# GpSimd waits for a gather's landing ahead of every third unit, and normalization batches of four up to the 44th unit, in a two-layer graph kernel

## The chip, the core and the metric

The kernel runs on one core of a Trainium2 chip. The metric is device time in microseconds (us) from start to end of one execution. Three runs of the kernel before took 1783.02, 1783.18 and 1783.73 us; the median is 1783.18 us. TensorE is written PE, VectorE DVE, ScalarE ACT, GpSimd POOL and SyncE SP, as in the profile.

## What is computed

There are 100,000 nodes with 128 features each and 50,000 edges, sorted by destination. Both layers normalize and clip the nodes' rows first.

```python
edge_index = jnp.stack([src, dst])
h = jnp.maximum(_layernorm(x, axis=-1), 0.0)
x = x + _L0_gnn_ref(h, relation_embedding, W1, b1, w2, edge_index, edge_type_200)
h = jnp.maximum(_layernorm(x, axis=-1), 0.0)
x = x + _L1_gnn_ref(h, src, dst)

# first layer, per edge and then per destination
triple = jnp.concatenate([x[src], x[dst], relation_embedding[edge_type]], axis=1)
c = triple @ W1 + b1
b = jax.nn.leaky_relu(c @ w2, SLOPE)
alpha = softmax of b over the edges of one dst
out = leaky_relu(segment_sum(c * alpha, dst))

# second layer: sum of feats[src] per dst, a node without edges keeps its own row
```

## The kernel before

The first layer goes through 261 units. A unit is three groups of 128 nodes (their rows are `xn`, loaded by SP, four units in one load) and up to two tiles of 128 edges. The source rows of the edges, `xe`, are fetched by POOL: `gather(u)` issues two indirect DMAs of 128 rows of 512 bytes for unit u (line 1112). `xe` has 16 slots, so `gather(u)` first waits until ACT has normalized unit u-16 (`L1.nrm`, line 1107).

All engines but POOL and SP walk through one loop of steps s, written out in full. Each issues its instructions strictly in the written order and meets the others by semaphores. In step s:

- DVE takes the statistics of some units further ahead (`stats`, line 1223; it waits for `x_in` and for `gathered`), makes the scalings of a batch once its last unit has been seen (`variances`, line 1231, and `ln_piece`, lines 1242, 1245, 1250, 1257), builds the selection matrices (`selT` 1310, `ot` 1320, `sel` 1333), runs the softmax of eight units in pieces, and adds the result to the nodes (1440, 1450).
- ACT copies messages out of PSUM (1562), makes the root of a batch's variances (`roots`, 1513 and 1515), normalizes unit s+2 (`norm`, five activations, 1527 and 1530), copies the turned tiles (1556) and unit s-15's sums (1568).
- PE turns unit s+1 (1601 to 1606), aggregates unit s-15 (1634 to 1637), and makes the messages of unit s (1618 to 1623).

The normalization batches are `LNB`: 2, 2, 4, 4 units, then thirty of 8, then 4, 2, 2, 1. `statistics_steps` spreads a batch's units over the steps between the end of the batch ahead and the step lo - 4, where lo is the batch's first unit. With batches of 8 behind each other the statistics of unit s+11 are taken in step s; with batches of 4 those of unit s+7. A gather can be at unit s+18 in step s, because of the 16 slots. At the very end the small batches ask for the last unit, 260, only in step 256.

SP brings `xn` and two tables every four steps and stores finished rows (lines 1006, 1026, 1038); these transfers and the gathers share the core's 16 DMA engines. The second layer begins when the first has stored all; it is not changed.

Of the kernel before, what the change touches and what calls it, by code (L numbers as in the profile page):

```python
# [16 lines left out]
def wait(engine, semaphore, value):  # L17

    if isinstance(value, int) and value <= 0:
        return  # L20
    engine.wait_ge(semaphore, value)
# [435 lines left out]
LB = 8  # L457
SB_ = 8
# [30 lines left out]
def gnn_two_layers(nc, x, src_e, dst_e, typ_e, rel, w1, b1, w2, out):  # L489
# [35 lines left out]
    with ctx:  # L525
# [95 lines left out]
        gathered = Ring(sem, "gathered", XE, 16 * UE)  # L621
# [63 lines left out]
        with ExitStack() as ctx1:  # L685
            block = ctx1.enter_context(nc.Block())

            @block.sync
            def _(sp):
                def first_x(q):  # L690
                    for rows_, g0, g1, np_ in parts_of(x, q):
                        sp.dma_start(xn[0:np_, q, g0:g1, :], rows_).then_inc(x_in.of(q), 16)

                for to, from_, landed in ((dsti, dst_e, k_dst), (srci, src_e, k_edge), (typi, typ_e, k_edge)):
                    sp.dma_start(to, from_.rearrange("o (p c) -> (o p) c", p=P)).then_inc(landed, 16)
                sp.dma_start(w1s[:, :, :], w1.rearrange("(a p) d -> p a d", p=P)).then_inc(k_in, 16)
                sp.dma_start(rels[:, 0, :], rel[0:P, :]).then_inc(k_in, 16)
                sp.dma_start(rels[0:RB, 1, :], rel[P:R, :]).then_inc(k_in, 16)
                sp.wait_ge(k_tab, 2)
                sp.dma_start(tab_d.rearrange("(p c) t -> p (c t)", p=P), tab.rearrange("p c t -> p (c t)")).then_inc(k_tabs, 16)  # L700
                sp.wait_ge(k_const, 1)
                sp.dma_start(nextp[0:P - 1, :], dst_e[:, EC:].rearrange("o (p c) -> (o p) c", c=EC)[:, 0:1],
                             allow_slow_non_contiguous=True).then_inc(k_in, 16)
                sp.dma_start(w2b[:, :], w2.partition_broadcast(P)).then_inc(k_in, 16)
                sp.dma_start(b1b[:, :], b1.partition_broadcast(P)).then_inc(k_in, 16)
                for k in range(TC):
                    sp.wait_ge(k_winl[1][k], 16)
                for q in range(2):
                    first_x(q)
                sp.wait_ge(k_places, UE)  # L710
                sp.dma_start(place_d.rearrange("(k p) s -> p k s", p=TU), plb).then_inc(k_out, 16)
                sp.wait_ge(k_types, UE)
                sp.dma_start(types_d.rearrange("(k p) s -> p k s", p=TU), tyb).then_inc(k_out, 16)
# [175 lines left out]
        with nc.If(flag == 0), ExitStack() as ctx2:  # L889
# [25 lines left out]
            def cut(sizes, most, total=NU):  # L915
                at, found = 0, []
                while at < total:
                    n = min(sizes[len(found)] if len(found) < len(sizes) else most, total - at)
                    found.append((at, at + n))
                    at += n  # L920
                return found

            def by_unit(batches):
                return {u: j for j, (lo, hi) in enumerate(batches) for u in range(lo, hi)}

            LNB, SMB = cut((2, 2, 4, 4) + 30 * (LB,) + (4, 2, 2, 1), LB), cut((), SB_)
            LN_OF, SM_OF = by_unit(LNB), by_unit(SMB)
            LNB2 = cut((1, 1, 2) + 30 * (LB2,) + (2, 1, 1), LB2, NU2)
            LN2_OF = by_unit(LNB2)
# [22 lines left out]
            def column(u, e):  # L952
                return (UE * (u // TU) + e) * TU + u % TU
# [4 lines left out]
            def xe_of(u):  # L958
                return xe[:, u % XE, :, :]
# [11 lines left out]
            def xe2_of(u):  # L971
                k = u % XE2
                return etiles[:, UT * k:UT * (k + 1), :] if k < 6 else xgroups[:, UT * (k - 6):UT * (k - 5), :]
# [4 lines left out]
            def tiles2(u):  # L978
                return UT - u % 2 - (u == NU2 - 1)
# [121 lines left out]
            @block.gpsimd  # L1101
            def _(pool):
                last_row = nc.gpsimd.to_reg(N - 1)

                def gather(u):
                    wait(pool, L1.nrm, u - XE + 1)
                    pool.sem_inc(turns, 1)
                    for e in range(UE):
                        if u < FIRST[e]:
                            continue  # L1110
                        j = column(u, e)
                        nc.gpsimd.indirect_dma_start(out=xe_of(u)[:, e, :], out_offset=None, in_=x,  # L1112
                                                     in_offset=bass.IndirectOffsetOnAxis(ap=idx_t[:, j:j + 1], axis=0),
                                                     bounds_check=last_row, oob_is_err=False
                                                     ).then_inc(gathered.of(u), 16)

                def gather2(u):
                    wait(pool, L2.y, u - XE2 + 2)
                    pool.sem_inc(turns, 1)
                    for k in range(tiles2(u)):  # L1120
                        j = NP2 * (u % 2 * UT + k) + u // 2
                        nc.gpsimd.indirect_dma_start(out=xe2_of(u)[:, k, :], out_offset=None, in_=x1_d,  # L1122
                                                     in_offset=bass.IndirectOffsetOnAxis(ap=idx2[:, j:j + 1], axis=0),
                                                     bounds_check=last_row, oob_is_err=False
                                                     ).then_inc(gathered.sems[u % XE2], 16)

                def window2(k):
                    if k == 0:
                        pool.wait_ge(k_borders, 2)
                    else:  # L1130
                        pool.wait_ge(k_rows2, k)
                    nc.gpsimd.indirect_dma_start(out=win2.rearrange("p c t -> p (c t)"), out_offset=None, in_=tab_d,
                                                 in_offset=bass.IndirectOffsetOnAxis(ap=at2[:, k:k + 1].bitcast(u32), axis=0)
                                                 ).then_inc(k_win2, 16)

                for u in range(NU):
                    if (u - T_WINDOW) % T_APART == 0 and 0 <= (u - T_WINDOW) // T_APART < ROUNDS:
                        window2((u - T_WINDOW) // T_APART)
                    gather(u)
                pool.wait_ge(s_c, NU)  # L1140
                nc.gpsimd.iota(row2, pattern=[[1, 4 * P]], base=0, channel_multiplier=0, allow_small_or_imprecise_dtypes=True
                               ).then_inc(k_row2, 1)
                for n in range(NQ - XS, NQ):
                    pool.wait_ge(stored.of(n), stored.count(n))
                pool.wait_ge(L1.nrm, NU)
                pool.wait_ge(k_tables2, ROUNDS)
                for u in range(NU2):
                    gather2(u)
# [608 lines left out]
```

## Time and profile before

| | |
|---|---|
| median of three runs | 1783.18 us |
| the profiled execution | 1799.49 us, its span 1795.3 us |
| busy over the span | PE 85%, DVE 82%, ACT 74%, POOL 65% |
| stretch 160 to 1000 us (224 units of the first layer) | PE 819.02 of 840 us, DVE 790.82, ACT 720.77, POOL 620.34 |
| granted TensorE clock | 1.00 in that stretch, 0.91 from 1100 to 1790 us |

Durations of rows are of the profiled execution. "Busy" of POOL leaves out the time between two instructions. A row of the timeline reads: start, duration, engine, line, operation, output<-input, count, and in brackets how long the engine had stood idle before it and what ended that.

### The profile page before, as it was taken

Reading aid. Unit: us, or ns where it says so; the run is one execution under the profiler, and the core shown is the slowest. Engines: PE = TensorE matmul, PEld = TensorE weight load, DVE = VectorE, ACT = ScalarE, POOL = GpSimd, SP = SyncE. Lnnn points to the kernel's source line nnn. Section 1 sums busy time; section 2 is a strip of 40 time slices with the busy share of each in tenths; the row PEclk is TensorE's granted clock in tenths of the full one; section 3 lists DMA queues with packets and bytes.
Section 4 is the critical chain, followed back from the end, with each engine's and each line's share of the span. In section 5 each row is a group of like instructions: output and inputs, shape, how many; then the busy total and the mean of one; then the engine's idle time right before and its main releaser. Section 6 shows DMA issues by size and latency. Waiting matters only on the chain.

```text
span 1795.3 us, 35038 instructions
## 1 busy us (share of the span) xinstructions
PE 1519.4 (85%) x12139; PEld 1346.7 (75%) x12139; DVE 1480.9 (82%) x4103; ACT 1335.6 (74%) x3492; POOL 1164.3 (65%) x994
## 2 busy tenths in 40 slices
PE   1379999999999999999999982687878778878787
PEld 0269999999999899998999982566656656656566
DVE  5548999999999899999999886677877787787786
ACT  0268888888888788888888952677766777777776
POOL 5756777777767677767777204666666666666661
PEclk9889999999999999999999996899899989989999
DMA  3543666666666566665666454477776677776754
GB/s 105 167 103 102 173 179 168 176 172 180 172 168 177 152 169 175 178 170 151 173 163 169 124 168 134 119 193 190 200 193 179 179 202 193 191 194 188 191 154 122
DMA packets 469368, 298.80 MB, mean 166 GB/s; under 512 B 35662, under 2 KB 438084, under 8 KB 469190
## 3 DMA queue, kind: packets, MB, share of 16 engines
q1 hardware_dynamic: 433942, 243.28, 49.2%
q0 software_dynamic: 35248, 53.28, 11.7%
q8 instruction: 95, 1.56, 0.4%
q14 instruction: 83, 0.68, 0.1%
HBM read 203.78 MB, written 104.34 MB: 172 GB/s over the span
## 4 chain that ended last, share of the span: by engine, by line
PE 47%; ACT 17%; POOL 10%; issue 9%; another core or an unknown queue 6%; DVE 5%; DMA 2%; SPq 0%; DVEq 0%; POOLq 0%; ACTq 0%
POOL xe L1122 8%; PE c_p L1618 5%; PE t_p L1604 5%; PE c_p L1619 5%; ACT an L1527 4%; ACT cs L1544 4%; PE c_p L1621 4%; PE t_p L1601 3%; ACT ae L1530 3%; PE t_p L1606 2%; PE t_p L1605 2%; PE y_p L1637 2%; ACT cs L1549 2%; PE y_p L1634 2%
## 5 line engine op out<-in xcount | busy, mean ns | idle before, releaser
L1112 POOL DMA_INDIRECT xe<-in_x,idx_t x516 | 681.6, 1321 | 264.6 <-issue 163.2
L1122 POOL DMA_INDIRECT xe<-x_d,idx x332 | 335.8, 1011 | 197.0 <-issue 128.2
L1223 DVE BATCH_NORM_STATS2 st<-xn 128x6 f32<-128x256 f32 x843 | 311.4, 413 | 39.4 <-DMA xn<-x_d,idx 27.2
L1527 ACT ACTIVATE an<-xn,nbias,rstd 128x128 f32<-128x128 f32 x783 | 326.9, 483 | 3.1 <-DVE nbias L1257 3.1
L1544 ACT ACTIVATE cs<-xn,nbias,rstd 128x128 f32<-128x128 f32 x782 | 310.3, 479 | 7.1 <-remote 7.1
L1223 DVE BATCH_NORM_STATS2 st<-xe 128x6 f32<-128x256 f32 x446 | 174.6, 412 | 108.0 <-DMA xe<-x_d,idx 96.2
L1530 ACT ACTIVATE ae<-xe,nbias,rstd 128x128 f32<-128x128 f32 x522 | 226.4, 483 | 0.0
L1618 PE MATMUL c_p<-w1a,th 128*128 128x129 f32 x1044 | 218.0, 290 | 9.9 <-issue 9.9
L1562 ACT ACTIVATE cs<-c_p 128x258 f32<-128x258 f32 x261 | 100.2, 384 | 147.6 <-remote 70.6
L1619 PE MATMUL c_p<-w1b,th 128*128 128x129 f32 x1044 | 203.8, 277 | 2.9 <-issue 2.9
L1333 DVE TENSOR_SCALAR sel<-row,plc_t,alpha 128x256 f32<-128x256 bf16 x522 | 194.3, 412 | 3.4
L1621 PE MATMUL c_p<-relk,ot 128*128 128x129 bf16 x1566 | 178.1, 222 | 2.4 <-issue 2.3
L1645 PE MATMUL y_p<-cs,ident 128*128 128x512 f32 x132 | 86.5, 791 | 97.0 <-issue 61.0
L1618 PEld LDWEIGHTS c_p<-w1a,th 128*128 128x128 f32 x1044 | 159.9, 193 | 10.7 <-issue 10.7
L1619 PEld LDWEIGHTS c_p<-w1b,th 128*128 128x128 f32 x1044 | 160.4, 194 | 3.1 <-issue 3.1
L1604 PE MATMUL t_p<-selT,an 128*128 128x256 f32 x522 | 159.8, 388 | 2.4 <-issue 1.1
L1556 ACT ACTIVATE th<-t_p 128x512 f32<-128x512 f32 x261 | 151.2, 579 | 9.5 <-remote 8.7
L1122 POOL DMA_INDIRECT xn<-x_d,idx x108 | 109.5, 1014 | 59.8 <-issue 29.6
L1601 PE MATMUL t_p<-ident,ae 128*128 128x128 f32 x522 | 105.8, 285 | 47.9 <-ACT ae L1530 41.8
L1568 ACT ACTIVATE lr<-y_p 128x390 f32<-128x390 f32 x261 | 126.0, 483 | 27.2 <-PE y_p L1637 22.5
L1549 ACT ACTIVATE cs<-xe,nbias,rstd 128x128 f32<-128x128 f32 x295 | 121.1, 480 | 33.4 <-DVE xn L1458 23.4
L1621 PEld LDWEIGHTS c_p<-relk,ot 128*128 128x128 bf16 x1566 | 133.8, 99 | 9.3 <-issue 2.4
(207 smaller groups left out, 3667.7 us busy)
## 6 DMA issues: line engine op xcount, KB each, us to landing
xn<-in_x SPq DMA_DIRECT2D x130, 384.0 KB
x_d<-xn SPq DMA_DIRECT2D x130, 384.0 KB
xn<-x_d SPq DMA_DIRECT2D x194, 256.0 KB
out<-xn SPq DMA_DIRECT2D x194, 256.0 KB
plr<-place_d SPq DMA_DIRECT2D x65, 256.0 KB
tyr<-types_d SPq DMA_DIRECT2D x65, 256.0 KB
xe<-in_x,idx_t POOLq DMA_INDIRECT x522
xe<-x_d,idx POOLq DMA_INDIRECT x332
```

Of the source, the lines that this page charges most:

```text
L1112: nc.gpsimd.indirect_dma_start(out=xe_of(u)[:, e, :], out_offset=None, in_=x, in_offset=bass.IndirectOffsetOnAxis(ap=idx_t[:, j:j + 1], ax ...
L1122: nc.gpsimd.indirect_dma_start(out=xe2_of(u)[:, k, :], out_offset=None, in_=x1_d, in_offset=bass.IndirectOffsetOnAxis(ap=idx2[:, j:j + 1], ...
L1223: return v.bn_stats(st[:, j % 2, c:c + 2, :].rearrange("p c t -> p (c t)"), rows_.rearrange("p r d -> p d r"))
L1333: last = v.tensor_scalar(sel[:, u % 4, e, :], row[:, :], plc_t[:, j:j + 1], alpha[:, k % 2, UE * at + e:UE * at + e + 1], ALU.is_equal, AL ...
L1527: a(an[:, u % 2, i, :], xs_of(u)[:, i, :], ACT.Relu, bias=nbias[:, j % 2, c:c + 1], scale=rstd[:, j % 2, c:c + 1])
L1530: last = a(ae[:, u % 2, e, :], xe_of(u)[:, e, :], ACT.Relu, bias=nbias[:, j % 2, c:c + 1], scale=rstd[:, j % 2, c:c + 1])
L1544: a(own2_[:, u % 3, g, :], xs2_of(u)[:, g, :], ACT.Relu, bias=nbias[:, j % 2, c:c + 1], scale=rstd[:, j % 2, c:c + 1])
L1601: tr(to[:, e * P:(e + 1) * P], ae[:, u % 2, e, :], ident[:, :])
L1604: mm(to[:, SLOTS:2 * SLOTS], an[:, u % 2, 1, :], one[:, P:3 * P], start=True, stop=False, skip_group_check=True)
L1618: mm(to, th[:, u % 2, e * P:(e + 1) * P], w1a[:, :], start=True, stop=False)
L1619: mm(to, th[:, u % 2, SLOTS + e * P:SLOTS + (e + 1) * P], w1b[:, :], start=False, stop=False)
L1621: mm(to, ot[:, u // QU % 2, 0, edges], relk[:, part_, :], start=False, stop=False)
```

## The change

Before a unit whose number divides by three POOL waits until both gathers of the unit ahead of it have landed in `xe`. And `LNB` has ten batches of four behind the first two of two, so that units 12 to 43 are eight batches of four and no longer four of eight; from unit 44 on the batches are the same.

```diff
-            LNB, SMB = cut((2, 2, 4, 4) + 30 * (LB,) + (4, 2, 2, 1), LB), cut((), SB_)
+            LNB, SMB = cut((2, 2) + 10 * (4,) + 26 * (LB,) + (4, 2, 2, 1), LB), cut((), SB_)
...
                 def gather(u):
+                    if u % 3 == 0 and u > 0:
+                        pool.wait_ge(gathered.of(u - 1), gathered.count(u - 1))
                     wait(pool, L1.nrm, u - XE + 1)
                     pool.sem_inc(turns, 1)
```

All lines of the kernel behind the second edit stand two further down. On POOL, where the slots are first used again: `nrm_1` is ACT's count of normalized units and `gathered1` the landing count of slot 1. Before, three units in a row:

```order
L1112 DMA xe<-in_x,idx_t 128x128 [waits nrm_1]
L1112 DMA xe<-in_x,idx_t 128x128
L1112 DMA xe<-in_x,idx_t 128x128 [waits nrm_1]
L1112 DMA xe<-in_x,idx_t 128x128
L1112 DMA xe<-in_x,idx_t 128x128 [waits nrm_1]
L1112 DMA xe<-in_x,idx_t 128x128
```

And now six units in a row, of which the third and the sixth divide by three:

```order
L1114 DMA xe<-in_x,idx_t 128x128 [waits nrm_1]
L1114 DMA xe<-in_x,idx_t 128x128
L1114 DMA xe<-in_x,idx_t 128x128 [waits nrm_1]
L1114 DMA xe<-in_x,idx_t 128x128
L1114 DMA xe<-in_x,idx_t 128x128 [waits gathered1,nrm_1]
L1114 DMA xe<-in_x,idx_t 128x128
L1114 DMA xe<-in_x,idx_t 128x128 [waits nrm_1]
L1114 DMA xe<-in_x,idx_t 128x128
L1114 DMA xe<-in_x,idx_t 128x128 [waits nrm_1]
L1114 DMA xe<-in_x,idx_t 128x128
L1114 DMA xe<-in_x,idx_t 128x128 [waits gathered4,nrm_1]
L1114 DMA xe<-in_x,idx_t 128x128
```

No instruction has moved; each sixth has a second wait, on the landing of what was issued directly before it.

On DVE, the statistics of units 12 to 15 (`gathered12` to `gathered15`) and what comes behind them. Before:

```order
L1223 BN_STATS st<-xn 128x6 [waits gathered15]
L1223 BN_STATS st<-xn 128x6
L1223 BN_STATS st<-xe 128x6
L1223 BN_STATS st<-xn 128x6 [waits gathered0,x_in4]
L1223 BN_STATS st<-xe 128x6
L1223 BN_STATS st<-xn 128x6 [waits gathered1]
L1223 BN_STATS st<-xn 128x6
L1223 BN_STATS st<-xe 128x6
```

And now:

```order
L1225 BN_STATS st<-xn 128x6 [waits gathered15]
L1225 BN_STATS st<-xn 128x6
L1225 BN_STATS st<-xe 128x6
L1233 TENSOR_SCALAR var<-st 128x42 [waits rstd_1,dve_1]
L1244 TENSOR_TENSOR tiny<-var,rstd 128x42 [waits rstd0_1]
L1279 SCALAR_TENSOR_TENSOR soft<-scn,s_p 16x128 [waits bT,scn_in0]
L1247 SCALAR_TENSOR_TENSOR tiny<-tiny,rstd 128x42 [waits dve_1]
L1252 SCALAR_TENSOR_TENSOR rstd<-tiny,rstd 128x42 [waits nrm_1,dve_1]
L1259 SCALAR_TENSOR_TENSOR nbias<-st,rstd 128x42 [waits dve_1]
L1225 BN_STATS st<-xn 128x6 [waits gathered0,x_in4]
```

A batch now ends behind unit 15: five DVE instructions for its scalings stand there, and the statistics of unit 16 (`gathered0`) come in step 9 and no longer in step 7, those of unit 19 in step 12 and no longer in step 8.

## Rows read from the trace of the kernel before

**Rows 1.** Windows, busy time of each engine (instructions), clock, DMA share.

```profile
core 0: us, PE busy (x) PEld busy (x) DVE busy (x) ACT busy (x) POOL busy (x), PEclk, DMA share, GB/s
160.00:1000.00 840.00, 819.02 (x7731) 788.60 (x7729) 790.82 (x2178) 720.77 (x1881) 620.34 (x453) 1.00 0.62 168
1100.00:1790.00 690.00, 543.88 (x3130) 414.93 (x3130) 519.28 (x1425) 491.08 (x1294) 439.81 (x435) 0.91 0.65 176
```

**Rows 2.** Lines, POOL, 160 to 1000 us: busy us, mean ns, idle before.

```profile
L1112 POOL DMA_INDIRECT xe<-in_x,idx_t x448 | 609.3, 1360 | 218.2 <-issue 136.4 <-ACT ae L1530 81.8
```

**Rows 3.** Lines, POOL, 1100 to 1790 us (second layer's gathers).

```profile
L1122 POOL DMA_INDIRECT xe<-x_d,idx x327 | 330.8, 1012 | 163.4 <-issue 94.5 <-remote 52.5 <-PE t_p L1655 7.2
```

**Rows 4.** Timeline, POOL: gathers whose landing ended an idle of DVE.

```profile
61.01 1.00 POOL L1112 DMA_INDIRECT xe<-in_x,idx_t  x1 [0.30 <-issue]
...
1115.18 1.00 POOL L1122 DMA_INDIRECT xe<-x_d,idx  x1 [0.30 <-issue]
...
1400.28 1.05 POOL L1122 DMA_INDIRECT xe<-x_d,idx  x1 [0.30 <-issue]
...
1743.68 1.05 POOL L1122 DMA_INDIRECT xn<-x_d,idx  x1 [0.30 <-issue]
```

**Rows 5.** Timeline, DVE: the instructions that waited for those gathers, in order.

```profile
67.41 0.76 DVE L1223 BATCH_NORM_STATS2 st<-xn 128x6 f32<-128x256 f32 x2 [2.58 <-DMA xe<-in_x,idx_t]
...
1117.67 0.43 DVE L1223 BATCH_NORM_STATS2 st<-xe 128x6 f32<-128x256 f32 x1 [2.65 <-DMA xe<-x_d,idx]
...
1406.08 1.10 DVE L1223 BATCH_NORM_STATS2 st<-xe 128x6 f32<-128x256 f32 x3 [4.29 <-DMA xe<-x_d,idx]
...
1746.94 0.76 DVE L1223 BATCH_NORM_STATS2 st<-xn 128x6 f32<-128x256 f32 x2 [0.51 <-DMA xn<-x_d,idx]
```

**Rows 6.** Timeline, POOL: the first layer's last gather.

```profile
998.85 3.07 POOL L1112 DMA_INDIRECT xe<-in_x,idx_t  x1 [0.30 <-issue]
```

**Rows 7.** Timeline, DVE: the variances of the first layer's last batch.

```profile
1046.17 0.18 DVE L1231 TENSOR_SCALAR var<-st 128x42 f32<-128x42 f32 x1
```

**Rows 8.** Lines, 160 to 1000 us: what one normalization batch costs DVE.

```profile
L1231 DVE TENSOR_SCALAR var<-st 128x42 f32<-128x42 f32 x28 | 6.5, 232 | 1.0
L1257 DVE SCALAR_TENSOR_TENSOR nbias<-st,rstd 128x42 f32<-128x42 f32 x28 | 5.9, 211 | 1.0
L1242 DVE TENSOR_TENSOR tiny<-var,rstd 128x42 f32<-128x42 f32 x28 | 5.7, 203 | 29.5 <-ACT rstd L1515 22.4 <-issue 6.9
L1250 DVE SCALAR_TENSOR_TENSOR rstd<-tiny,rstd 128x42 f32<-128x42 f32 x28 | 5.1, 183 | 0.0
L1245 DVE SCALAR_TENSOR_TENSOR tiny<-tiny,rstd 128x42 f32<-128x42 f32 x28 | 4.6, 165 | 0.0
```

**Rows 9.** Lines, ACT, 160 to 1000 us: its batch pair, and its idle.

```profile
L1562 ACT ACTIVATE cs<-c_p 128x258 f32<-128x258 f32 x225 | 86.4, 384 | 111.7 <-remote 53.3 <-PE c_p L1623 43.6 <-issue 13.0
...
L1515 ACT ACTIVATE rstd<-lnv 128x42 f32<-128x42 f32 x28 | 6.7, 239 | 0.9
L1513 ACT ACTIVATE lnv<-var 128x42 f32<-128x42 f32 x28 | 6.5, 232 | 0.0
```

**Rows 10.** Timeline, POOL: the second layer's first gather.

```profile
1093.02 1.01 POOL L1122 DMA_INDIRECT xe<-x_d,idx  x1 [32.41 <-issue]
```

## The prediction

> **What bounds the kernel now.** I read the windows first, for who is busy in the stretch that the change touches; then the lines of POOL there, for how much room it has; then pairs of a gather and the DVE instruction that waited for it, for how long a landing takes; last the end of the first layer, for how far POOL is ahead there.
>
> From 160 to 1000 us PE is busy 819.02 of 840 us [rows 1]: PE paces the first layer, and nothing that leaves PE alone can give back more than the 21 us in which it idles. The stretch holds 448 gathers, so 224 units, 3.75 us each. DVE is busy 790.82 us, ACT 720.77, POOL 620.34.
>
> POOL's 620 looks like room for a third more, and is not. Each of its 448 gathers lasts 1.36 us, together 609.3 us, and in front of each stand about 0.30 us in which it issues [rows 2, 4]. That is 448 x 0.30 = 134.4 us of the 218.2 us of idle. What is left is 83.8 us, nearly all of it (81.8 us) idle that ended when ACT had normalized a unit. So POOL is really free for 83.8 / 224 = 0.374 us in each unit, 1.12 us in three.
>
> **The landing wait.** POOL waits for the unit that it has issued directly before, so it pays the whole time from the end of the last gather instruction to its landing. The views of before give no landing time for these gathers, but DVE shows it where it had to wait for one. The gather of unit 7 ended at 61.01 + 1.00 = 62.01, the statistics that needed it began at 67.41: 5.40 us. In the second layer, with gathers of the same size and a like DMA share (0.65 against 0.62, [rows 1]), the pairs shown are 1117.67 - 1116.18 = 1.49 us, 1406.08 - 1401.33 = 4.75 us and 1746.94 - 1744.73 = 2.21 us [rows 4, 5]. The trace has 54 such pairs, of which the first and the last are shown; they lie between 1.46 and 5.40 us with a mean of 3.15 us. They lean to the late side, since only a late landing makes DVE wait; the second layer's wait is for a whole unit's last gather, as here. I take 3.1 us, near their mean. Each wait takes the place of one 0.30 us gap, so it costs POOL 2.8 us net.
>
> Queued behind the waiting instruction on POOL are all later gathers and the window gathers of the second layer's tables; who waits for them is DVE (the statistics), then ACT, then PE.
>
> The sum, for the 240 units from about unit 20 on, where the slots are in use again (80 waits):
>
> - waits: 80 x 2.8 = 224 us added to POOL;
> - room: 240 x 0.374 = 90 us;
> - lead: the last gather ends at 998.85 + 3.07 = 1001.9 us [rows 6], lands some 3 us later, and is asked for by the variances of the last batch at 1046.17 us [rows 7]. POOL may so fall 41 us behind before the end of the layer moves;
> - 224 - 90 - 41 = 93 us;
> - relief: a gather lasts 1.36 us here and 1.01 us in the second layer [rows 2, 3]. The 0.35 us more, 480 x 0.35 = 168 us over the 240 units, I put down to DVE's work, which is denser here; if the same DVE work is spread over about a tenth more time, a tenth of that goes: 17 us off.
>
> That leaves +76 us. In words: POOL's own time for three units goes from 3 x 3.75 - 1.1 = 10.1 to 12.9 us, less the relief about 12.7, against PE's 11.2 us. POOL becomes the bound of the first layer at about 4.2 us per unit, and PE, ACT and DVE all show holes. The decisive point is where 80 x (landing - 0.30) equals 90 + 41 us: a mean landing of 1.94 us. Below it nothing is lost, above it each 0.1 us costs 8 us.
>
> The Trainium skill speaks against this sum. "DMA: Bandwidth & Descriptors", section "Anatomy of one DMA — SWDGE (gpsimd) path", gives a transfer started by GpSimd a nearly constant 2.0 us from issue to completion plus its bytes by the bandwidth. By that a 64 KB gather would have landed about 1.2 us behind the end of a 1.0 us instruction, the waits would add 80 x 0.9 = 72 us, less than the room, and the sum would be 0. The trace disagrees in its mean (3.15 us), and agrees only with its shortest pairs (1.46 us).
>
> **The ramp.** The first 16 units wait for no slot and are issued back to back; the new wait stands in that run five times, from unit 3 on. Unit 7 is one for which DVE waited there already (2.58 us, [rows 5]). I count nothing extra for the ramp: POOL stands idle for ACT right behind it, for a slot, and the bounds below are far wider.
>
> **The batches of four.** Four batches more. One batch costs DVE 0.232 + 0.211 + 0.203 + 0.183 + 0.165 = 0.99 us of work and 29.5 / 28 = 1.05 us of idle ahead of line 1242 [rows 8], and ACT 0.239 + 0.232 = 0.47 us [rows 9]. If all of it were on the path: 4 x 2.5 = 10 us. What hides it: DVE idles 840 - 790.8 = 49 us in 28 batches, 1.76 us for each eight units, and ACT more (111.7 us of idle ahead of its first instruction of a step, [rows 9]). The other side: statistics are taken for unit s+7 and not s+11, so a late gather hurts four units later, but only up to unit 43; POOL's total is the same whatever DVE does. I take 0 where POOL is the bound, since its lateness covers it, and +4 (0 to +10) where it is not.
>
> **Against the profiled execution.** 1799.5 us + 76 = 1875.5 us, with a span of about 1871. The runs without the profiler are 16.3 us shorter (1783.2 against 1799.5), so 1859 us.
>
> **Rivals.**
>
> - *POOL keeps up.* The landings that POOL waits for come early, because with at most six gathers under way less stands in the queue ahead of them. For it: the 1.49 us pair, and that the pairs lean to the late side. Against it: the other three pairs, and a DMA share of 0.62, so that at most moments something else is being moved. With 1.5 us: 80 x 1.2 = 96 us against 131 of room and lead, so nothing is lost, and the time is 1783 + 0 to 10 for the batches, 1785 us. That is also the case in which the landing is over before the wait is reached. The rule of the skill above gives this time.
> - *Faster: fewer gathers under way, and PE's stalls shrink.* 23 times ACT waits for PE's messages with no releaser seen, 53.3 us in all [rows 9]: PE is late there for a reason the profile doesn't name, and if that is transfers crowding each other, holding gathers back could help. Its place is these stalls, its price at most PE's idle, 21 us in this stretch; I take half, 10 us: 1773 us. It decides only if the mean landing stays under 1.94 us. Against it: the same bytes are moved, and SP's large loads, not the gathers, make most of the DMA share.
> - *Much slower: late landings, and the clock.* POOL waits on average 4.0 us, because its waits end up in the middle of SP's bursts: 80 x 3.7 = 296 - 131 - 20 = +145 us, 1928 us. With it, or instead of it, the clock: where PE is busy 543.88 of 690 us its granted clock is 0.91, where it is busy 819 of 840 it is 1.00 [rows 1]. A first layer at 4.2 us per unit has PE busy 84% or so, and stretches at the lower level (1.2 GHz) may appear there. Most of that would fall into PE's new holes, since POOL sets the pace; I put +0 to +50 us on it.
>
> **How the numbers follow.** The forecast (POOL is the bound, landing 2.4 to 3.8 us, so +20 to +132 us) has 0.62; much slower 0.15; POOL keeps up 0.16; faster 0.07. The time is 1859 us; its own range, from 2.4 to 3.8 us of landing, is 1803 to 1915. The range for 8 in 10 reaches down to no change, 1783, and up to 1930, to the 4.0 us case; left out are the faster case and the worst of the slow one. About 0.2% (3.6 us) is what a measurement of this kernel can tell from no change. Slower by more than that: 0.62 + 0.15 + 0.04 (POOL keeps up, but the batches cost 4 to 10 us) = 0.81. Within it: 0.12. Faster: 0.07.
>
> **What would show it right or wrong.** Right: in the lines of POOL, every sixth gather has an idle of some 3 us ahead of it, ended by a landing, and the idle ended by ACT is nearly gone; DVE's statistics of `xe` wait for DMA or POOL; PE's busy share of the first layer falls to about 85%; a unit takes about 4.2 us from unit 60 on; the second layer's length is as before. The batches would show as four more instructions of the kind of line 1231 before 250 us, with no pause of PE at them. Wrong in size: the mean idle ahead of the sixth gather is far from 3 us. Wrong in kind: POOL still idles for ACT at most units, and the second layer's first gather stays near 1093 us [rows 10]; then the landing wait is mostly over when it is reached. If the time is lost elsewhere, in the ramp before 160 us or in the second layer, the argument fails whatever the total.

## The result, and the profile after

The changed kernel takes 1971.7 us where the kernel before takes 1783.1 us on the same chip: the ratio is 1.106, with an interval of 1.102 to 1.109, so about 185 to 189 us slower. Of the four executions behind the 1971.7 us, three took 1966.5, 1967.6 and 1975.9 us, and the fourth, a slow one with a granted TensorE clock of 0.60, took 2395.3 us and tells nothing of the change. The forecast was 1859 us, at most 1930. Profiled against profiled, which is what a sum from rows can be held to, it is 1975.9 against 1799.5 us, +176 us where the sum said +76. The side was right and the size was not.

The windows of the profile after, to be held against [rows 1]; the first lies in the first layer, the second in the second layer:

```profile
core 0: us, PE busy (x) PEld busy (x) DVE busy (x) ACT busy (x) POOL busy (x), PEclk, DMA share, GB/s
160.00:1200.00 1040.00, 882.79 (x7797) 841.56 (x7796) 804.35 (x2216) 737.51 (x1902) 594.94 (x464) 0.93 0.51 137
1290.00:1970.00 680.00, 544.14 (x3130) 418.22 (x3130) 517.01 (x1416) 490.18 (x1292) 438.03 (x432) 0.91 0.66 179
```

PE's share fell from 97.5% to 85% and its granted clock from 1.00 to 0.93, while the second layer is as it was: from the end of the first layer to the end of the kernel it takes 730 us and took 739. All of the loss is in the first layer. The gathers there, from the lines of POOL between 160 and 1180 us (to be held against [rows 2]):

```profile
L1114 POOL DMA_INDIRECT xe<-in_x,idx_t x451 | 570.1, 1264 | 436.0 <-DMA xe<-in_x,idx_t 269.5 <-issue 118.7 <-ACT ae L1532 47.8
```

451 gathers now take 1020 us, so 4.52 us for a unit; it was 3.75. Their idle doubled, and the largest part of it is ended by a landing. The waits of the same stretch (engine, tile and line, what was waited for: us in total, times, longest) show who inherits it:

```profile
POOL xe L1114 <- DMA xe<-in_x,idx_t: 269.5, 61, 10.9
DVE st L1225 <- DMA xe<-in_x,idx_t: 175.7, 60, 12.3
PEld t_p L1606 <- DVE selT L1312: 125.5, 38, 11.1
POOL xe L1114 <- issue: 120.8, 378, 5.9
PE t_p L1606 <- DVE selT L1312: 116.1, 34, 10.9
ACT cs L1564 <- PE c_p L1625: 113.2, 136, 2.2
ACT th L1558 <- PE t_p L1608: 95.3, 29, 10.2
POOL xe L1114 <- ACT ae L1532: 54.2, 20, 6.6
```

POOL waits for its own landings, DVE's statistics for the same landings, PE for DVE, ACT for PE. The chain that ended last says the same: it was PE 47% and POOL 10% before, and is now

```profile
POOL 25%; PE 20%; issue 18%; DMA 16%; DVE 7%; ACT 7%; another core or an unknown queue 3%; POOLq 0%; SPq 0%; DVEq 0%
DMA xe<-in_x,idx_t 15%; POOL xe L1114 11%; POOL xe L1124 10%; POOL xn L1124 3%; ACT an L1529 2%; PE t_p L1606 2%; PE c_p L1620 2%; PE y_p L1657 2%; PE t_p L1657 2%; PE c_p L1657 2%; ACT cs L1546 2%; PE c_p L1621 1%; DVE st L1225 1%; PE y_p L1647 1%
```

**One wait, row by row.** POOL's timeline (start, length; idle before and its releaser in brackets), with three waits, two ended by landings and one put down to ACT:

```profile
509.36 1.00 POOL L1114 DMA_INDIRECT xe<-in_x,idx_t  x1 [0.30 <-issue]
510.66 1.53 POOL L1114 DMA_INDIRECT xe<-in_x,idx_t  x1 [0.30 <-issue]
512.49 1.00 POOL L1114 DMA_INDIRECT xe<-in_x,idx_t  x1 [0.30 <-issue]
518.15 1.01 POOL L1114 DMA_INDIRECT xe<-in_x,idx_t  x1 [4.66 <-DMA xe<-in_x,idx_t]
...
534.36 1.16 POOL L1114 DMA_INDIRECT xe<-in_x,idx_t  x1 [6.55 <-ACT ae L1532]
...
541.69 0.99 POOL L1114 DMA_INDIRECT xe<-in_x,idx_t  x1 [0.30 <-issue]
549.11 0.99 POOL L1114 DMA_INDIRECT xe<-in_x,idx_t  x1 [6.43 <-DMA xe<-in_x,idx_t]
```

At the second one the landing came at 533.54, and the gather began 0.82 us later: the wait is for the landing, and ACT is named only because its count rose between the two. The last one has a witness, since DVE waited for the same landing:

```profile
548.38 0.43 DVE L1225 BATCH_NORM_STATS2 st<-xn 128x6 f32<-128x256 f32 x1 [2.31 <-DMA xe<-in_x,idx_t]
```

The gather ended at 541.69 + 0.99 = 542.68; the last part of its data came at 548.28 (semaphore record), DVE began 0.10 us later, POOL 0.83 us later. So a wait has two prices, the landing and POOL's **restart**. Over all 80 waits from unit 21 to unit 258 the landing is 3.48 us behind the end of the gather in the mean (3.10 predicted), and the restart is 0.82 us in 78 of them (not predicted). The last 0.05 us come from the other two: at unit 216 a gather of the second layer's tables (a "window gather", line 1134) stands between and ends after the landing, and at unit 231 POOL starts 2.31 us behind it, for a reason that the trace doesn't show. Together 4.36 us from the end of the gather ahead to the start of the waited one (ten under 2.3, the longest 10.9), in place of a gap of 0.30: net 4.06 us and not 2.8. The idle alone is 4.27 us, since two window gathers of 2.5 and 4.1 us run inside these stretches.

**The bookkeeping**, from the first gather of unit 20 to that of unit 260, by adding up the gaps between the gathers of `xe` and their lengths. A gap is the time from the end of one to the start of the next, so that the five window gathers of the stretch lie in the gaps, before and after:

| term | predicted | measured |
|---|---|---|
| 80 waits, net | +224 | 80 x 4.06 = +325 |
| room used | -90 | -101 |
| gathers shorter (1.336 to 1.262 us, 480 of them) | -17 | -35 |
| ahead of unit 20 (100 to 117 us) | 0 | +17 |
| last unit's gather starts later (997 to 1202 us) | | +205 (terms: +206) |
| lead recovered by the layer's end (1060.0 to 1245.6 us) | -41 | -20 |
| second layer and tail | 0 | -9 |
| time of the profiled execution | +76 | +176 |

### The profile page after: what moved, and what is told of

It is laid out like the page before. It is cut to its first block, busy times and chain, and to the rows that moved or that the text cites. A ratio compares the mean times of both kernels' runs of the same rounds, so it can differ in the third digit from the quotient of the medians.

```text
span 1971.9 us, 35078 instructions
## 1 busy us (share of the span) xinstructions
PE 1572.5 (80%) x12139; PEld 1394.5 (71%) x12139; DVE 1487.2 (75%) x4123; ACT 1345.7 (68%) x3500; POOL 1128.5 (57%) x994
## 3 DMA queue, kind: packets, MB, share of 16 engines
q8 instruction: 95, 1.56, 0.3%
## 4 chain that ended last, share of the span: by engine, by line
POOL 25%; PE 20%; issue 18%; DMA 16%; DVE 7%; ACT 7%; another core or an unknown queue 3%; POOLq 0%; SPq 0%; DVEq 0%
DMA xe<-in_x,idx_t 15%; POOL xe L1114 11%; POOL xe L1124 10%; POOL xn L1124 3%; ACT an L1529 2%; PE t_p L1606 2%; PE c_p L1620 2%; PE y_p L1657 2%; PE t_p L1657 2%; PE c_p L1657 2%; ACT cs L1546 2%; PE c_p L1621 1%; DVE st L1225 1%; PE y_p L1647 1%
## 5 line engine op out<-in xcount | busy, mean ns | idle before, releaser
L1114 POOL DMA_INDIRECT xe<-in_x,idx_t x516 | 643.2, 1247 | 504.2 <-DMA xe<-in_x,idx_t 304.1
L1606 PE MATMUL t_p<-selT,an 128*128 128x256 f32 x522 | 171.6, 412 | 123.5 <-DVE selT L1312 119.3
L1620 PE MATMUL c_p<-w1a,th 128*128 128x129 f32 x1044 | 225.4, 299 | 1.3 <-issue 1.0
L1621 PE MATMUL c_p<-w1b,th 128*128 128x129 f32 x1044 | 209.1, 283 | 0.0
L1606 PEld LDWEIGHTS t_p<-selT,an 128*128 128x128 f32 x522 | 83.1, 201 | 134.4 <-DVE selT L1312 129.5
L1620 PEld LDWEIGHTS c_p<-w1a,th 128*128 128x128 f32 x1044 | 167.8, 202 | 1.3 <-issue 0.8
L1621 PEld LDWEIGHTS c_p<-w1b,th 128*128 128x128 f32 x1044 | 166.6, 201 | 0.4 <-issue 0.4
L1515 ACT ACTIVATE lnv<-var 128x42 f32<-128x42 f32 x78 | 18.4, 236 | 185.8 <-issue 106.8
```

The costliest lines, as they stand in the source:

```text
L1606: mm(to[:, SLOTS:2 * SLOTS], an[:, u % 2, 1, :], one[:, P:3 * P], start=True, stop=False, skip_group_check=True)
L1620: mm(to, th[:, u % 2, e * P:(e + 1) * P], w1a[:, :], start=True, stop=False)
L1621: mm(to, th[:, u % 2, SLOTS + e * P:SLOTS + (e + 1) * P], w1b[:, :], start=False, stop=False)
```

## The experiments

They ran on three more chips, so each is held against before on its own chip. On two of them before is faster, 1666.5 us; there a unit takes 3.53 us and not 3.74, and POOL's room is only 58 to 61 us in 240 units (102 to 112 on the others, all by the count above, window gathers included). "Gap" below is that from the end of the gather ahead to a waited gather, in the mean; "shift" is by how much the last unit's gather starts later than in a profile of the same chip in which POOL waits for no landing: the batches alone for the first three rows, the thin tables without the wait for the next three, the wait eight units back for the last two. The shift is no test, since it is a sum over the same rows; what is tested are the gaps, and that the time follows the shift. The shift is of one profiled execution, the time of the median; for phase 1 the profiled execution took 1892.9 us and the other three 1852 to 1868, so its row is of a longer execution than its time.

| kernel | waits x net | relief, room, ramp | shift | time |
|---|---|---|---|---|
| wait alone | 80 x 3.78 = 302 | -36 -47 +20 | 240 | +227 |
| wait for unit u-2 | 80 x 2.00 = 160 | -10 -47 +8 | 112 | +99 |
| every sixth unit | 40 x 4.18 = 167 | -25 -47 +8 | 104 | +76 |
| one in four, phase 1 | 60 x 4.01 = 240 | -44 -84 +13 | 126 | +88 |
| one in four, phase 2 | 60 x 5.99 = 359 | -63 -93 +15 | 218 | no ratio |
| wait, thin tables | 80 x 3.40 = 272 | -44 -91 +19 | 156 | +125 |
| changed kernel again | 80 x 3.95 = 316 | -46 -50 +24 | 245 | +226 |
| wait alone again | 80 x 3.93 = 314 | -37 -50 +21 | 248 | +232 |

**The two edits apart.** The wait with the batches of before, and the batches without the wait:

```diff
+                    if u % 3 == 0 and u > 0:
+                        pool.wait_ge(gathered.of(u - 1), gathered.count(u - 1))
```

> The landing wait alone, batches as before. Theory A (POOL's own time is the loss, 80 waits of 4.36 us idle each in the changed kernel, where I had counted 3.1): 1960 to 1975 us, the whole loss. Rival B (the batches of four are part of the loss that I had not counted, since DVE idles for them too): 1880 to 1940 us.

```diff
-            LNB, SMB = cut((2, 2, 4, 4) + 30 * (LB,) + (4, 2, 2, 1), LB), cut((), SB_)
+            LNB, SMB = cut((2, 2) + 10 * (4,) + 26 * (LB,) + (4, 2, 2, 1), LB), cut((), SB_)
```

> The batches of four alone, no landing wait. Theory A: they cost 0 to 10 us, 1787 us, because POOL is not the bound here and four batches are 4 x 2.5 us at most. Rival B: a good part of the 110 us that my sum missed, so 1830 us or more.

The wait alone: 1893.5 us, ratio 1.139 (1.135 to 1.143). The batches alone: 1667.2 us, 1.0000 (0.998 to 1.002). The wait is the whole loss. (The times that were expected are those of the first chip; on this one, with before 116 us shorter and half the room, only the ratios and differences can be held against them.) To see whether the batches matter once POOL is the bound, the changed kernel and the wait alone ran again on one chip:

> The changed kernel again, beside the kernel with its wait alone on the same chip. Theory (wait alone makes the loss): the ratio to before is 1.10 to 1.14 according to how fast before is on this chip, and within 0.5% of that of the wait alone. Rival (with GpSimd as the bound the batches of four cost or save something that they don't on top of the kernel before): more than 0.5% (9 us) apart from the wait alone.

> The wait ahead of every third unit with the batches of before. Theory: same time as the changed kernel on this chip to within 0.5%; the mean gap ahead of the 80 waited gathers is 4.0 to 4.4 us in both. Rival: the batches matter under the wait, and the two differ by more than 9 us.

1892.0 us, ratio 1.137 (1.133 to 1.141), and 1898.0 us, 1.142 (1.137 to 1.147), with mean gaps of 4.25 and 4.23 us. They are 6 us (0.3%) apart and their intervals overlap: no effect of the batches shows here either.

**An older landing.** POOL waits for the unit before the last:

```diff
+                    if u % 3 == 0 and u > 1:
+                        pool.wait_ge(gathered.of(u - 2), gathered.count(u - 2))
```

> Batches as before; ahead of every third unit POOL waits for the landing of the unit two back, not of the one directly ahead. Theory A: issuing the unit between takes 3.3 us, so of a mean landing of 3.5 us little is left; about half the waits still find something to wait for, 80 x 1.3 = 104 us against 131 us of room and lead: 1783 to 1795 us. Rival (what costs is having the gathers' queue kept short, or the wait instruction itself): most of the loss stays, over 1880 us.

1766.2 us, ratio 1.063 (1.059 to 1.066). I missed this one: +12 us at most was expected, and +99 came. The landings waited for come 4.34 us behind the end of their gather, of which the next unit takes up 3.24, so the means alone leave 1.1 us. But the landings spread, a late one is paid and an early one gives nothing back, and each wait that really waits, 59 of the 80, pays the restart: the mean gap is 2.30 us, 2.00 net. And 131 us of room and lead were to cover that, as on the first chip; this one has 58 us of room.

**Half as many waits.** `u % 6 == 0` in place of `u % 3 == 0`:

```diff
+                    if u % 6 == 0 and u > 0:
+                        pool.wait_ge(gathered.of(u - 1), gathered.count(u - 1))
```

> Batches as before; the wait for the landing of the unit directly ahead stands ahead of every sixth unit, so 40 waits on the stretch and not 80. Theory A, with the price per wait of the changed kernel (4.36 - 0.30 = 4.06 us) and room plus lead of 131 us: 40 x 4.06 = 162 - 131 = +31 us, less relief: 1795 to 1815 us. Rival (each wait costs the same share, no room or lead): half the loss, 1875 us.

1742.4 us, ratio 1.046 (1.043 to 1.048). The price of one wait stayed (4.48 us of gap), the number of them halved, and what is left of 167 us behind the room is +76. So the loss is not half but a third of that of the wait alone: the room is taken off once. The expected time is missed all the same, +12 to +32 us against +76: it took off 131 us of room and lead, as on the first chip.

**Is it the wait instruction, or waiting?** The same 80 waits, on landings eight units old:

```diff
+                    if u % 3 == 0 and u > 7:
+                        pool.wait_ge(gathered.of(u - 8), gathered.count(u - 8))
```

> GpSimd waits ahead of every third unit, but for the landing of the unit eight before, about 30 us earlier; the batches are as before. Theory (each wait costs what it really waits for, plus 0.82 us from the release to the next gather in place of the 0.30 us gap): nothing is waited for, so the 80 gaps stay near 0.30 us, and the time is within 5 us of before (ratio 0.998 to 1.003). Rival (the wait instruction itself stops GpSimd's issue, and the 0.52 us are its price): 80 x 0.52 = 42 us, which the room of 55 to 100 us swallows, so the time is near before too, but the 80 gaps show 0.82 us. The rows of the gaps tell the two apart, not the time.

1666.5 us, ratio 1.0003 (0.999 to 1.0015), and the median gap ahead of the waited gathers is 0.30 us. A wait that finds its count already there costs POOL nothing; the restart belongs to true waiting. (The mean gap, 0.52 us, holds two window gathers and the few waits for ACT's slots that fall on these units.)

**Where the landing falls against SP's transfers.** In the trace after, the landings that POOL waits for depend on the unit's number modulo four, and SP starts a bundle of table loads, feature loads and stores every four units. So the wait was put once in four units, at two phases, ahead of units 4k+1 and of units 4k+2:

```diff
+                    if u % 4 == 1:
+                        pool.wait_ge(gathered.of(u - 1), gathered.count(u - 1))
```

> Batches as before; the landing wait ahead of every fourth unit, the units 4k+1, so that POOL always waits for unit 4k. The units 4k end furthest behind SP's bundle of loads and land soonest in the kernels without waits (1.95 and 2.37 us in two traces). Theory A (loss = waits x (landing + 0.82 us restart - 0.30 us) - POOL's room - the lead at the end - relief): 60 x 2.7 = 162 us, less 54 to 107 of room, 28 of lead, 15 of relief: +10 to +65 us over the kernel before of the same chip. Rival (the phase against SP's transfers is of no matter, only the count of waits): 60 x (3.9 + 0.5) = 265, so +115 to +160 us.

```diff
+                    if u % 4 == 2:
+                        pool.wait_ge(gathered.of(u - 1), gathered.count(u - 1))
```

> As the run with 4k+1, with the same number of waits, but ahead of the units 4k+2, so that POOL always waits for unit 4k+1, the one that ends just as SP's bundle begins (landings of 5.04 and 4.52 us in the two traces). Theory A: 60 x 5.3 = 318 us, less 54 to 107, 28 and 25: +160 to +210 us. Rival (only the count of waits matters): the same as the run with 4k+1.

Phase 1 takes 1867.9 us, ratio 1.047 (1.042 to 1.052), with a mean gap of 4.31 us; phase 2 between 1929 and 1979 us, too scattered for a ratio, with 6.29 us; the shortest execution of phase 2 is 36 us longer than the longest of phase 1. Three window gathers lie in the gaps of phase 2 and none in those of phase 1; the idle alone is 6.14 against 4.31 us. So the same number of waits, one unit further on, costs 1.82 us more each, 109 us of POOL's time. The mean landing is 5.43 us against 3.46. (Each profile is of the longest of the four executions of its kernel.) The timelines show one wait of each. Phase 1, POOL and then SP:

```profile
507.16 1.00 POOL L1114 DMA_INDIRECT xe<-in_x,idx_t  x1 [0.30 <-issue]
510.71 0.99 POOL L1114 DMA_INDIRECT xe<-in_x,idx_t  x1 [2.55 <-DMA xe<-in_x,idx_t]
```

```profile
511.30 0.35 SPq L1026 DMA_DIRECT2D plr<-place_d  x1
511.69 0.43 SPq L1026 DMA_DIRECT2D tyr<-types_d  x1
```

Phase 2, the same:

```profile
506.53 1.00 POOL L1114 DMA_INDIRECT xe<-in_x,idx_t  x1 [0.30 <-issue]
514.05 1.00 POOL L1114 DMA_INDIRECT xe<-in_x,idx_t  x1 [6.52 <-ACT ae L1532]
```

```profile
504.16 0.33 SPq L1026 DMA_DIRECT2D plr<-place_d  x1
504.54 0.43 SPq L1026 DMA_DIRECT2D tyr<-types_d  x1
505.02 1.02 SPq L1006 DMA_DIRECT2D xn<-in_x  x2
```

In phase 1 the gather ended 3.1 us ahead of SP's loads and had landed 1.7 us later. In phase 2 it ended 3.4 us behind their start and took 5.7 us (6.52 less the restart; the record names ACT, but nearly every such gap of this kernel is the landing plus 0.82). Sorted by the nearest start of the table loads, the gather ends 0 to 9 us behind it in 59 of the 60 waits of phase 2, with a mean landing of 5.50 us. In phase 1 it does so in 28 waits, 4.70 us, and ends up to 9 us ahead in 31, with 2.20 us within 4 us and 2.58 us beyond. The waits of the changed kernel are: 16 that end within 4 us ahead of the loads, 1.56 us; 13 that end 4 to 9 us ahead, 2.35 us; 47 that end up to 9 us behind their start, 4.38 us; 4 in neither.

Phase 1 missed its forecast too, +88 us where +10 to +65 was expected. That was worked out from landings of about 2 us, as the units 4k have them where POOL doesn't wait; with the wait in place half of the gathers fell behind the start of the loads, and the mean was 3.46. A wait moves its engine against the other queue's bursts, so landings read without it don't carry over. Phase 2 was expected at +160 to +210 us and its executions lie at +150 to +199.

**Thin tables.** SP's two table loads cut from the third on to 16 columns, so that the rest of each table is left out, with the wait and without it:

```diff
+                    wide = (hi - lo) * SLOTS if q < TB else 16
...
-                        sp.dma_start(to[:, q % TB, 0:(hi - lo) * SLOTS],
-                                     table[lo:hi, :].rearrange("g s -> (g s)").partition_broadcast(P)
+                        sp.dma_start(to[:, q % TB, 0:wide],
+                                     table[lo:hi, :].rearrange("g s -> (g s)")[0:wide].partition_broadcast(P)
```

> The landing wait of the change, batches as before, and SP's two table loads of four units cut to 16 columns from the third on (this leaves out the contents of the tables, so selections are of old data). Theory A with transfers of SP as what delays a landing: the mean landing falls from 3.3 us to 2 us or less, 80 x 1.3 = 104 us of the loss goes, so +100 to +140 us are left over the kernel before with the same cut. Rival (a landing is late for its own rows and not for SP's loads): the loss stays at +200 us or more.

> The kernel before with the same cut of SP's table loads (their contents are left out). It is the base for the run with the wait and the cut. Theory A: PE paces the first layer, so no change within 10 us, and the landings are shorter in the trace. Rival (PE and DVE are held back by SP's loads): faster by over 20 us.

Without the wait 1777.4 us, ratio 0.999 (0.997 to 1.001): the table loads as such cost nothing where POOL doesn't wait for a landing. With it 1902.5 us, ratio to before 1.069 (1.067 to 1.071), and +125 us over the same cut without the wait; +100 to +140 was expected, from landings of 2 us or less. The windows of both, 160 to 960 us, without and with the wait:

```profile
160.00:960.00 800.00, 786.93 (x7438) 758.60 (x7435) 760.10 (x2096) 692.72 (x1809) 595.04 (x438) 1.00 0.50 137
```

```profile
160.00:960.00 800.00, 717.63 (x6470) 684.66 (x6468) 660.90 (x1812) 609.46 (x1580) 476.92 (x379) 0.96 0.43 119
```

The landings waited for take 2.81 us in place of the 3.2 to 3.5 us with full tables (on other chips). The gain is where the gather ends up to 9 us behind the start of the loads, 3.41 us in place of 4.17 to 4.38, and not ahead of them, 1.57 us in place of 1.51 to 1.59. So the table loads are part of the landing time and not most of it; that the rest is the feature loads and stores, which remain, is not shown.

## Why the prediction was wrong

- **Who is the bound.** Right. POOL sets the pace, PE is busy 85% as predicted, and DVE, ACT and PE wait in a row behind the landing, the second layer is unchanged.
- **The price of a wait: the step that failed.** The sum had "2.8 us net". It is 4.06: 0.38 us from the landing (3.48 for 3.10), 0.82 us from the restart, 0.05 us from units 216 and 231. That is +101 us, about the 100 by which the sum was short. It is luck that the other terms don't show: they were off by -11, -18, +17, +21 and -9 us, which cancel. "Each wait takes the place of one 0.30 us gap" took for granted that the next gather starts at the moment of the landing. The landing's error cost 30 us; the restart alone 66.
- **The restart stood in the trace of before.** There POOL truly waited for ACT, and ACT's end is shown: `ae` of 409.65 us ended at 410.52 and the gather began at 411.32, 0.80 us later. Over the 66 idle times longer than 0.8 us between units 21 and 260 the median from ACT's last end to the gather is 0.81 us. POOL's row and ACT's row, which were not read beside each other:

```profile
411.32 1.42 POOL L1112 DMA_INDIRECT xe<-in_x,idx_t  x1 [1.62 <-ACT ae L1530]
```

```profile
409.65 0.87 ACT L1530 ACTIVATE ae<-xe,nbias,rstd 128x128 f32<-128x128 f32 x2
```

- **Landing times.** The 54 pairs had a mean of 3.15 us, and 3.48 came. They were near, in part by luck: the number is no constant, but 1.6 us or 4.4 us by where the gather ends against SP's loads. The rule of the Trainium skill that the prediction weighed ("DMA: Bandwidth & Descriptors", section "Anatomy of one DMA — SWDGE (gpsimd) path") asks for a landing about 1.2 us behind a 1.0 us gather. The trace comes near it at the 16 waits that end just ahead of SP's loads (1.56 us), and not in the mean of the 80 (3.48 us).
- **The room.** Right: the idle beyond 0.30 us in front of the gathers that wait for no landing fell from 97 us to 2, 90 predicted. (The 101 us of the table hold two window gathers too, which after the change are counted with the waits.) POOL waits for ACT's slots no more; the 54 us that the list of waits puts down to ACT are waits for landings.
- **Lead.** Predicted 41 us, recovered 20. The lead was read at the last batch, which holds one unit, and the tightest batch is the last one of eight. In before its variances are asked for at 987.78 us, and the last gather that they need ended at 964.79 + 1.22 = 966.0:

```profile
964.79 1.22 POOL L1112 DMA_INDIRECT xe<-in_x,idx_t  x1 [0.30 <-issue]
```

```profile
987.78 0.28 DVE L1231 TENSOR_SCALAR var<-st 128x42 f32<-128x42 f32 x1
```

That leaves 987.8 - 966.0 - 3.1 = 18.7 us. After the change the same gather ended at 1167.2 and the variances began at 1170.72, 3.6 us later: no lead is left there, while the one unit of the last batch still has 24 us.
- **Relief.** Predicted 17 us, measured 35: the gathers became shorter as DVE's share fell from 94% to 77%. The amount was half; a tenth more time was put in, and the layer grew by a sixth. That DVE's work is the cause is not shown: across the runs the two don't go in step, for in phase 1 and phase 2 the gathers are shorter still (1.236 and 1.196 us) and DVE is busier (84% and 79%).
- **Ramp.** Predicted 0, measured 17. Six waits stand ahead of unit 20 (units 3 to 18), and nothing covers enough of them: at unit 20 POOL is 17 us behind. It is not made good, for POOL is the bound from then on.
- **Batches.** Right: no change by themselves (1.0000), and none to be seen with the wait.
- **Clock.** The granted clock did fall, to 0.93 in the first layer. No run here changes the clock alone, so what it costs is not separated; PE idles 157 us in that stretch, and the gathers' rows account for the loss without it.
- **Rivals.** "POOL keeps up" needed landings below 1.94 us, by its own account; with the restart the point is 1.94 - 0.82 = 1.12 us, and the shortest of the 80 took 1.35. "Much slower" had the right cause, waits in the middle of SP's bursts, but with 4.0 us too long a landing (3.48) and no restart: 3.7 us net, the nearest of the rivals to the 4.06 measured. With the restart added it would have come to 80 x 4.52 = 362 us against 325.

Left open: why before is 7% faster on two of the chips, what the feature loads and the stores each add to a landing, and why the gathers became shorter.

## What to carry to other kernels

A wait on the landing of the transfer just issued costs its engine the landing, plus a restart, minus one gap; read the restart off any true wait of that engine in the trace of before, by the end of the releaser against the start of the released, before pricing a new one. A late engine has as much lead as the tightest consumer leaves it, and here that is the last large batch and not the last one. Landing times read where the engine doesn't wait are a first guess only, because the wait shifts it against the other queues' bursts. And take the room off once, with the room of the chip that runs it.

## What the hardware showed beyond that

- GpSimd needs 0.82 us from the semaphore to the start of the next gather after a true wait, on four chips alike, and leaves a gap of 0.30 us to the gather ahead where it did not have to wait, be a wait there or not.
- DVE started 0.10 us after the landing that released POOL after 0.83 us.
- A gather of 128 rows of 512 bytes lands 1.5 to 1.6 us behind its end in the mean (2.2 in phase 1) where it ends within 4 us ahead of SP's bundle of loads, and 4.2 to 5.5 us where it ends up to 9 us behind their start; moving a wait by one unit changed the mean idle from 4.31 to 6.14 us.
- The same program took 1666 us on two chips and 1780 to 1783 us on two others.
